# Issuing a state-space part's on-chip copies from ScalarE's queue instead of the sync engine's

## The chip, the cores and the metric

The kernel runs on one core of a Trainium2 chip. TensorE (PE) multiplies matrices into PSUM; VectorE (DVE), ScalarE (ACT) and GpSimd (POOL) do the elementwise work; SyncE (SP) computes nothing and here issues transfers. Every engine has an instruction queue of its own that it takes in order, and they meet only at semaphores. The metric is the time of one execution on the device in microseconds (us), the median of three runs.

## The reference, cut to what matters

The input is x of shape (8, 256, 128) after normalisation over the last axis. Two branches start from it and are multiplied at the end:

```python
xn = layernorm(x)
s = mamba_block(xn)                     # selective state space, D = 256 channels, N = 16 states
g = silu(local_transformer(xn))         # 6 layers, 16 heads, windows of 32 tokens, gelu feed-forward
x = x + s * g

# inside mamba_block, for each batch entry
delta = softplus(dbc[:DTR] @ dup_W + dup_b)
A_disc = exp(delta[..., None] * A)
B_x = delta[..., None] * Bm[:, :, None, :] * x1[..., None]
hc = A_disc[t] * hc + B_x[t]            # over 256 time steps
y = einsum('tbdn,btn->btd', hs, Cm)
```

## The kernel before, in words

There are 48 attention steps s: six layers over eight batch entries, each of 256 tokens. The loop `for i in STEADY` (i = 1 to 46) is written once for every engine, as a list of calls in a fixed order; a call such as `copy_p(i, 2)` works on step i and waits on semaphores for what it needs. A call whose step is not in range does nothing.

The state-space part is spread over the same loop. It works on one batch entry in every six steps (`is_batch`: s = 0, 6, ..., 42), eight in all. Its calls stand in the list at fixed lags, so that `z_bu(i - 3, 0)` acts only in steps i = 3, 9, 15, ..., 45. For one batch the sequence is:

- ACT copies the projections to `dbc` (`z_copy_dbc`), and POOL makes `du`, which holds delta and delta times x1 (`z_delta`).
- `replicate_bc(s, 0)` copies four groups of eight rows of `dbc` (the B and C rows) into partitions 0 to 7 of `BC`; `replicate_bc(s, 1)` to `(s, 4)` double them to 16, 32, 64 and 128 partitions. Each of these waits for the one before.
- `replicate(s, n)`, n = 0 to 7, copies sixteen rows of `du` into one of four buffers `rep`, each row into eight partitions. It waits for `delta_done` and, where the buffer was used before, until the decays and products that read it are done.
- Sixteen chunks j follow, two from each replication: ACT makes the decay `exp(delta A)` (`z_decay`), POOL the product with B (`z_bu`, line 1862), DVE the scan (`z_scan`), POOL the product with C (`z_hc`), PE the sum (`z_sum`). Chunk 0 of POOL also waits for all of `BC`.

In the kernel before, all transfers are on SP's queue. `spread` (line 539) copies pieces of V and `arrange_x` (line 553) rearranges x for the values; both wait for ACT or PE. The `replicate` and `replicate_bc` calls stand among them.

Of the attention part these calls bear on what follows, all in the order of the engine's list. On PE: `turn` and `turn_p` transpose q, k and the probabilities (`turn_p`, line 775, waits for POOL's `normalise_p`), `scores` and `values_out` use them, `w_gelu` and `w_gate` are the feed-forward products. On ACT: `copy_qk`, `copy_p`, `copy_o` and `copy_v` empty PSUM, `square` and `expo` feed the norms and the softmax, `gelu` feeds the feed-forward part. On POOL: `rotate_sum`, `normalise` and `normalise_p`. POOL's list for a step in which a batch starts has, near its end,

```python
z_bu(i - 3, 0)
z_bu(i - 3, 1)
rotate_sum(i + 1, 5)
normalise_p(i, 2)
z_bu(i - 3, 2)
rotate_sum(i + 1, 6)
z_bu(i - 3, 3)
normalise_p(i, 3)
```

with calls between them that do nothing in that step.

Of the kernel before, what the change touches and what calls it, by code (L numbers as in the profile page):

```python
# [21 lines left out]
NB, SEQ, DM = 8, 256, 128  # L22
# [354 lines left out]
def main_phase(nc, t, k, R2, T, C0, X, M, Y):  # L377

    with ExitStack() as ctx:
# [145 lines left out]
        def _(sp):  # L525
# [72 lines left out]
            def replicate_bc(s, n):  # L598

                if not is_batch(s):  # L600
                    return
                b = s // BSTEP
                if n == 0:
                    sp.wait_ge(dbc_copied, b + 1)
                    if b > 0:
                        sp.wait_ge(hc_done, 16 * b)
                    for z in range(2):
                        for h in range(2):
                            r = DTR + z * NST + 8 * h
                            sp.dma_start(BC[0:8, z, h, :], dbc[r:r + 8, :]).then_inc(bc_in, 16)  # L610
                else:
                    sp.wait_ge(bc_in, BC_IN * b + 64 + 16 * (n - 1))
                    r = 8 << (n - 1)
                    sp.dma_start(BC[r:2 * r], BC[0:r]).then_inc(bc_in, 16)

            def replicate(s, n):

                if not is_batch(s):
                    return
                b = s // BSTEP  # L620
                sp.wait_ge(delta_done, b + 1)
                k = 8 * b + n - NREP
                if k >= 0:
                    chunks = 16 * (k // 8) + 8 * (k % 8 // 4) + 5 + k % 4
                    sp.wait_ge(dA_done, chunks)
                    sp.wait_ge(bu_done, chunks)
                r = ROWS16[n]
                sp.dma_start(rep[:, (8 * b + n) % NREP].rearrange("p z c t -> p (z c t)"),
                             du[r::8].rearrange("d (o z) c t -> d o (z c t)", o=1).broadcast_to([16, 8, 2 * DBLK * SEQ]))\
                  .then_inc(rep_in[(8 * b + n) % NREP], 16)  # L630

# [12 lines left out]
            for i in STEADY:  # L644
                replicate(i - 6, 6)
# [3 lines left out]
                replicate(i - 3, 1)  # L649
# [3 lines left out]
                replicate_bc(i - 3, 0)  # L653
                replicate_bc(i - 3, 1)
                next_qk(i + 1, 0)
                replicate(i - 3, 2)
                replicate_bc(i - 3, 2)
                replicate_bc(i - 3, 3)
                replicate(i - 2, 0)
# [1441 lines left out]
```

## Time and profile before

| what | value |
|---|---|
| median of three runs | 1753.79 us (1752.3 to 1754.01) |
| the profiled execution's own time | 1751.25 us |
| span of the profile | 1749.2 us |
| PE busy | 1683.9 us, 96% |
| DVE busy | 1525.0 us, 87% |
| POOL busy | 1406.8 us, 80% |
| ACT busy | 1251.7 us, 72% |
| mean share of TensorE's clock granted | 0.994 |

The span runs from the first instruction to the last of the profiled execution; its own time includes what lies around it. Busy time of an engine counts its arithmetic; semaphores and the issuing of transfers are not in it. PE's busy time is a modelled one, since its matmuls are pipelined.

### The profile page before, as it was taken

The page shows a single profiled execution, that of the slowest core. Times are in us where ns is not written, and L with a number is a line of the kernel's source. Part 1 is how long each engine was busy: PE and PEld are TensorE (multiplying, and loading weights), DVE is VectorE, ACT ScalarE, POOL GpSimd, SP SyncE. Part 2 cuts the span into 40 slices and gives each one's busy share as a digit, 9 for nine tenths or more (in the row PEclk, how much of TensorE's full clock was granted, in tenths as well). Part 3 has the DMA queues.
Part 4 walks back from the last instruction along what each step waited for, and adds up shares of the span by engine and source line. Part 5 has one row for each costly group of instructions (what it writes and reads, how often), then busy time and mean ns, then how long its engine had stood idle before and what let it go on. Part 6 is the DMA issues. An engine that isn't in the chain of part 4 may idle for free.

```text
span 1749.2 us, 73908 instructions
## 1 busy us (share of the span) xinstructions
PE 1683.9 (96%) x30944; PEld 980.9 (56%) x30944; DVE 1525.0 (87%) x2751; ACT 1251.7 (72%) x2328; POOL 1406.8 (80%) x1265
## 2 busy tenths in 40 slices
PE   5899999999999999999999999999999999999987
PEld 2555555555556555555555555555555565556552
DVE  7878898989988999889889898898898989988976
ACT  4657677677786777866877668767677677786764
POOL 3777888878888887988889778897888888888872
PEclk9999999999999999999999999999999999999998
DMA  5213232232213322132421323214231242212340
GB/s 141 49 36 85 61 79 54 63 84 53 62 36 84 80 66 54 34 90 54 102 65 35 83 52 75 75 37 94 48 83 30 64 107 66 48 36 54 75 96 24
DMA packets 96694, 114.18 MB, mean 65 GB/s; under 512 B 42398, under 2 KB 62636, under 8 KB 96364
## 3 DMA queue, kind: packets, MB, share of 16 engines
q1 hardware_dynamic: 96364, 109.46, 26.3%
q8 instruction: 246, 4.03, 1.0%
q14 instruction: 84, 0.69, 0.1%
HBM read 19.22 MB, written 1.05 MB: 12 GB/s over the span
## 4 chain that ended last, share of the span: by engine, by line
PE 72%; DVE 14%; issue 4%; POOL 3%; SPq 2%; ACT 2%; DMA 2%; POOLq 0%; DVEq 0%; ACTq 0%
PE bank L713 14%; PE bank L797 9%; PE bank L738 9%; PE bank L729 8%; PE bank L814 7%; PE bank L758 6%; PE bank L775 5%; PE bank L842 3%; PE bank L857 3%; DVE qn L1490 3%; DVE qc L1490 3%; PE bank L866 2%; DVE ssq L1497 2%; PE bank L750 2%; PE bank L921 2%
## 5 line engine op out<-in xcount | busy, mean ns | idle before, releaser
L1817 POOL TENSOR_TENSOR AB<-qc,qn 128x512 f32<-128x512 f32 x384 | 487.9, 1276 | 116.7 <-DVE qn L1490 115.4
L1828 POOL TENSOR_TENSOR AB<-AB,rinv 128x512 f32<-128x512 f32 x384 | 392.0, 1045 | 31.8 <-DVE rinv L1515 31.8
L713 PE MATMUL bank<-wqkv,XT 128*128 128x512 f32 x768 | 380.2, 596 | 7.1 <-DVE qn L1490 4.9
L1835 POOL TENSOR_TENSOR Pb<-Pb,p_rden 128x512 f32<-128x512 f32 x192 | 200.8, 1046 | 144.0 <-DVE p_rden L1536 141.6
L1127 ACT ACTIVATE qkT<-bank 128x512 f32<-128x512 f32 x384 | 228.8, 596 | 107.3 <-PE bank L738 105.6
L1118 ACT ACTIVATE sq<-bank 128x512 f32<-128x512 f32 x384 | 228.5, 595 | 95.7 <-PE bank L713 95.5
L1490 DVE TENSOR_TENSOR qc<-bank,rt 128x512 f32<-128x512 f32 x384 | 258.6, 673 | 9.2 <-ACT sq L1118 7.3
L1497 DVE TENSOR_REDUCE ssq<-sq 128x8 f32<-128x512 f32 x384 | 258.1, 673 | 6.0 <-ACT sq L1118 5.2
L1490 DVE TENSOR_TENSOR qn<-bank,rt 128x512 f32<-128x512 f32 x384 | 261.5, 681 | 0.0
L797 PEld LDWEIGHTS bank<-PT,V 64*64 64x64 f32 x12288 | 196.9, 134 | 94.4 <-issue 89.8
L738 PE MATMUL bank<-ident,AB 128*128 128x128 f32 x1536 | 242.7, 280 | 3.7 <-ACT qkT L1127 3.3
L738 PEld LDWEIGHTS bank<-ident,AB 128*128 128x128 f32 x1536 | 173.7, 140 | 123.0 <-issue 85.1
L797 PE MATMUL bank<-PT,V 64*64 64x32 f32 x12288 | 217.9, 220 | 4.3 <-ACT PT L1142 2.4
L1142 ACT ACTIVATE PT<-bank 128x512 f32<-128x512 f32 x192 | 114.1, 594 | 147.1 <-PE bank L775 144.8
L1522 DVE TENSOR_REDUCE mx<-bank 128x8 f32<-128x512 f32 x192 | 131.2, 684 | 93.2 <-PE bank L758 92.5
L729 PE MATMUL bank<-wqkv,XV 128*128 128x512 f32 x384 | 191.2, 599 | 2.4 <-DVE qn L1490 2.4
L1605 DVE TENSOR_TENSOR_SCAN hb<-bank,hb 128x256 f32<-128x256 f32 x256 | 161.4, 672 | 33.3 <-ACT bank L1302 33.3
L814 PE MATMUL bank<-OT,wo 128*128 128x512 f32 x384 | 180.6, 593 | 0.0
L1862 POOL TENSOR_TENSOR hb<-rep,BC 128x512 f32<-128x512 f32 x128 | 163.3, 1282 | 12.2 <-DMA rep<-du 4.3
L713 PEld LDWEIGHTS bank<-wqkv,XT 128*128 128x128 f32 x768 | 127.1, 191 | 79.2 <-issue 68.3
L758 PE MATMUL bank<-qkT 64*32 64x64 f32 x12288 | 164.0, 222 | 3.9 <-issue 3.9
L1134 ACT ACTIVATE Pb<-Pb 128x512 f32<-128x512 f32 x192 | 120.8, 629 | 59.2 <-DVE Pb L1525 58.9
(145 smaller groups left out, 2492.5 us busy)
## 6 DMA issues: line engine op xcount, KB each, us to landing
V<-V SPq DMA_DIRECT2D x672, 64.0 KB
rep<-du SPq DMA_DIRECT2D x64, 512.0 KB, 4.7
wqkv<-in_Wqkv SPq DMA_DIRECT2D x36, 256.0 KB, 3.2
XV<-XT SPq DMA_DIRECT2D x96, 64.0 KB, 2.1
wo<-in_Wo SPq DMA_DIRECT2D x6, 512.0 KB, 5.3
BC<-BC SPq DMA_DIRECT2D x8, 256.0 KB
w<-in_W SPq DMA_DIRECT2D x6, 341.0 KB, 4.5
xin<-in_x SPq DMA_DIRECT2D x4, 256.0 KB, 4.1
```

The source lines that it names most:

```text
L713: pe.matmul(R[u % 2][:], XT[:, s % NB, (u % 2) * P:(u % 2 + 1) * P], wqkv[:, (u // 2) * 512:(u // 2 + 1) * 512], start=True, stop=True).th ...
L729: pe.matmul(R[n % 2][:], XV[:, q % 2, s % 2, tl, :], wqkv[:, c:c + 512], start=True, stop=True)\
L738: mm = pe.transpose(T[:, c * P:(c + 1) * P], AB[:, (8 * s + u) % NAB, c * P:(c + 1) * P], ident[:])
L758: mm = pe.matmul(SB[w * WIN:(w + 1) * WIN, odd, col:col + 2 * WIN], qkT[p0:p0 + DH, g % 2, c, WIN + tok:2 * WIN + tok], qkT[p0:p0 + DH, g ...
L797: mm = pe.matmul(o_bank(s)[DH * odd:DH * (odd + 1), tl, c * P + w * WIN:c * P + (w + 1) * WIN], V[r, w, h0:h0 + DH], PT[r, g % 2, 2 * odd ...
L814: mm = pe.matmul(c_bank("w_out", s), wo[:, k, :], flat(OT[:, k]), start=k == 0, stop=k == 7)
L1118: act.activation(sq[:, u % 2, :], R[u % 2][:], ACT.Square).then_inc(sq_done, 1)
L1127: act.activation(qkT[:, g % 2, :, WIN + tl * P:WIN + (tl + 1) * P], T.rearrange("p (c t) -> p c t", c=4), ACT.Copy).then_inc(qkT_done, 1)
L1490: ins = dve.tensor_tensor(out if z == 0 else out[:, :, :, ::-1, :], src, tab, ALU.mult)
L1497: dve.reduce_sum(ssq[:, 8 * u:8 * u + 8, 0], sq[:, u % 2, :].rearrange("p (h d) -> p h d", d=DH), AX_X)\
L1817: pool.tensor_tensor(AB[:, n % NAB, :], qc[:, u % 2, :], qn[:, u % 2, :], ALU.add).then_inc(rs_done, 1)
L1828: pool.tensor_tensor(o, o, r, ALU.mult).then_inc(nm_done, 1)
```

## The change

The functions `replicate_bc` and `replicate` move from SP's block to ACT's, with `sp` replaced by `act` and nothing else altered. Their calls leave SP's list and are placed in ACT's list, at the positions shown; the waits that they begin with are now in ACT's queue. The lists of PE, DVE and POOL are unchanged.

```diff
 SP's loop
             for i in STEADY:
-                replicate(i - 6, 6)
                 next_qk(i, 1)
                 next_qk(i, 2)
                 spread(i, 0)
-                replicate(i - 3, 1)
                 next_v(i, 0)
                 next_qk(i, 3)
                 spread(i, 1)
-                replicate_bc(i - 3, 0)
-                replicate_bc(i - 3, 1)
                 next_qk(i + 1, 0)
-                replicate(i - 3, 2)
-                replicate_bc(i - 3, 2)
-                replicate_bc(i - 3, 3)
-                replicate(i - 2, 0)
-                replicate(i - 6, 7)
                 spread(i, 2)
-                replicate_bc(i - 3, 4)
                 spread(i, 3)
                 arrange_x(i + 1)
-                replicate(i - 5, 5)
-                replicate(i - 4, 4)
-                replicate(i - 3, 3)
                 next_v(i, 1)
                 other_weights(i)
 ACT's block
+            def replicate_bc(s, n):
+
+                if not is_batch(s):
+                    return
+                b = s // BSTEP
+                if n == 0:
+                    act.wait_ge(dbc_copied, b + 1)
+                    if b > 0:
+                        act.wait_ge(hc_done, 16 * b)
+                    for z in range(2):
+                        for h in range(2):
+                            r = DTR + z * NST + 8 * h
+                            act.dma_start(BC[0:8, z, h, :], dbc[r:r + 8, :]).then_inc(bc_in, 16)
+                else:
+                    act.wait_ge(bc_in, BC_IN * b + 64 + 16 * (n - 1))
+                    r = 8 << (n - 1)
+                    act.dma_start(BC[r:2 * r], BC[0:r]).then_inc(bc_in, 16)
...
 ACT's loop
                 copy_v(i, 2)
+                replicate(i - 6, 6)
                 z_decay(i - 8, 14)
                 copy_v(i, 3)
                 z_decay(i - 5, 5)
                 copy_qk(i, 2)
                 expo(i, 0)
+                replicate(i - 3, 1)
                 square(i + 1, 0)
                 copy_qk(i, 3)
                 z_tap(i + 2)
                 z_decay(i - 6, 9)
                 scale_x(i - 3)
                 square(i + 1, 1)
+                replicate_bc(i - 3, 0)
                 z_copy_dbc(i - 1)
                 z_decay(i - 8, 15)
                 copy_p(i, 0)
                 square(i + 1, 2)
+                replicate_bc(i - 3, 1)
                 expo(i, 1)
                 gelu(i - 3, 0)
                 copy_qk(i, 4)
                 square(i + 1, 3)
+                replicate(i - 3, 2)
                 gelu(i - 3, 1)
                 copy_qk(i, 5)
+                replicate_bc(i - 3, 2)
                 copy_o(i, 0)
                 square(i + 1, 4)
                 gelu(i - 3, 2)
                 z_copy_g(i - 4)
+                replicate_bc(i - 3, 3)
                 z_decay(i - 4, 3)
                 copy_p(i, 1)
                 square(i + 1, 5)
+                replicate(i - 6, 7)
                 expo(i, 2)
                 copy_qk(i, 6)
+                replicate_bc(i - 3, 4)
                 square(i + 1, 6)
                 z_copy_dx(i - 1)
                 copy_o(i, 1)
+                replicate(i - 2, 0)
                 copy_qk(i, 7)
...
                 z_decay(i - 4, 4)
+                replicate(i - 5, 5)
                 z_softplus(i - 1)
                 copy_p(i, 2)
+                replicate(i - 4, 4)
                 expo(i, 3)
                 z_decay(i - 3, 0)
+                replicate(i - 3, 3)
```

After the loop the last batch's `replicate` calls 5, 6 and 7 move likewise, behind `copy_qk(LAST, 5)`, `copy_qk(LAST, 7)` and `expo(LAST, 3)`.

## Rows read from the trace of the kernel before

**Rows 1.** The profile page: busy time by engine, and the chain's shares.

```profile
PE 1683.9 (96%) x30944; PEld 980.9 (56%) x30944; DVE 1525.0 (87%) x2751; ACT 1251.7 (72%) x2328; POOL 1406.8 (80%) x1265
...
PE 72%; DVE 14%; issue 4%; POOL 3%; SPq 2%; ACT 2%; DMA 2%; POOLq 0%; DVEq 0%; ACTq 0%
```

**Rows 2.** POOL's waits: engine, line, waited for: us in total, times, longest.

```profile
POOL hb L1862 <- DMA rep<-du: 4.3, 5, 1.3
...
POOL hb L1862 <- DMA BC<-BC: 2.0, 1, 2.0
```

**Rows 3.** Instructions of tiles rep and BC: ns min/median/max, first and last start.

```profile
L628 SPq DMA_DIRECT2D rep<-du x64: 529/572/1876, 117.5 to 1696.1; - x64
...
DMA to landing us min/median/max: 4.3/4.7/5.9
...
L610 SPq DMA_DIRECT2D BC<-dbc x32: 624/649/1146, 142.2 to 1614.2; - x32
```

**Rows 4.** Busy time by engine in step 21: stretch, its length, us busy, clock.

```profile
769.20:803.20 34.00, 33.74 (x645) 19.98 (x646) 29.15 (x53) 26.05 (x47) 26.75 (x25) 1.00 0.45 99
```

**Rows 5.** SP's timeline, end of step 21: start us, us, instruction.

```profile
785.00 0.59 SPq L614 DMA_DIRECT2D BC<-BC  x1
...
792.79 0.56 SPq L628 DMA_DIRECT2D rep<-du  x1
```

**Rows 6.** Instructions of tile BC in step 21: first and last start.

```profile
L610 SPq DMA_DIRECT2D BC<-dbc x4: 624/644/682, 772.3 to 774.4; - x4
L614 SPq DMA_DIRECT2D BC<-BC x4: 507/608/1551, 776.2 to 785.0; - x4
```

**Rows 7.** POOL's timeline, end of step 21, with idle time before and releaser.

```profile
788.67 2.53 POOL L1862 TENSOR_TENSOR hb<-rep,BC 128x512 f32<-128x512 f32 x2 [0.73 <-issue]
...
792.36 1.06 POOL L1835 TENSOR_TENSOR Pb<-Pb,p_rden 128x512 f32<-128x512 f32 x1
...
797.18 1.27 POOL L1862 TENSOR_TENSOR hb<-rep,BC 128x512 f32<-128x512 f32 x1 [1.29 <-DMA rep<-du]
798.46 1.04 POOL L1835 TENSOR_TENSOR Pb<-Pb,p_rden 128x512 f32<-128x512 f32 x1
```

**Rows 8.** Line 1141's semaphore (the first wait of copy_p) on ACT's queue, 774 to 780.

```profile
L1141 ACTq EVENT_SEMAPHORE  x1: 17/17/17, 775.4 to 775.4; - x1
```

**Rows 9.** ACT's timeline in step 21.

```profile
776.53 0.59 ACT L1118 ACTIVATE sq<-bank 128x512 f32<-128x512 f32 x1
777.68 0.60 ACT L1142 ACTIVATE PT<-bank 128x512 f32<-128x512 f32 x1 [0.56 <-PE bank L775]
...
779.03 0.62 ACT L1134 ACTIVATE Pb<-Pb 128x512 f32<-128x512 f32 x1
...
780.97 0.69 ACT L1200 ACTIVATE ge<-bank,vecs 128x512 f32<-128x512 f32 x1
...
789.52 0.60 ACT L1127 ACTIVATE qkT<-bank 128x512 f32<-128x512 f32 x1 [0.38 <-PE bank L738]
...
795.45 0.60 ACT L1142 ACTIVATE PT<-bank 128x512 f32<-128x512 f32 x1 [1.96 <-PE bank L775]
796.66 0.63 ACT L1134 ACTIVATE Pb<-Pb 128x512 f32<-128x512 f32 x1 [0.62 <-DVE Pb L1525]
797.20 0.86 ACT L1302 ACTIVATE bank<-rep,Aneg 128x256 f32<-128x256 f32 x2
```

**Rows 10.** PE's timeline in step 21.

```profile
781.71 1.12 PE L842 MATMUL bank<-xc,w 128*128 128x512 f32 x2
...
794.75 0.66 PE L775 MATMUL bank<-ident,Pb 128*128 128x128 f32 x4
...
799.84 0.66 PE L775 MATMUL bank<-ident,Pb 128*128 128x128 f32 x4
```

**Rows 11.** Two stretches early in the span: length, us busy, clock as in rows 4.

```profile
97.30:100.70 3.40, 1.30 (x66) 1.22 (x67) 2.79 (x8) 2.25 (x7) 1.04 (x1) 1.00 0.10 23
100.70:104.10 3.40, 3.40 (x8) 1.80 (x8) 0.12 (x1) 1.68 (x3) 3.20 (x4) 0.50 0.25 59
```

More of the change, by code:

```diff
@@ L596, in store @@
                              written(p).rearrange("p (i n) -> p i n", n=DM)).then_inc(stored, 16)
[L598 to L630, printed above, removed]
             def take_state():
@@ L674, in _ @@
             spread(LAST, 3)
-            replicate(LAST_B, 5)
-            replicate(LAST_B, 6)
-            replicate(LAST_B, 7)
             reload_x()
@@ L1161, in copy_v, with replicate @@
                    .then_inc(v_copied, 1)
+            def replicate_bc(s, n):
[14 more added lines that the diff above has]
+                    act.dma_start(BC[r:2 * r], BC[0:r]).then_inc(bc_in, 16)
+            def replicate(s, n):
+                if not is_batch(s):
+                    return
+                b = s // BSTEP
+                act.wait_ge(delta_done, b + 1)
+                k = 8 * b + n - NREP
+                if k >= 0:
+                    chunks = 16 * (k // 8) + 8 * (k % 8 // 4) + 5 + k % 4
+                    act.wait_ge(dA_done, chunks)
+                    act.wait_ge(bu_done, chunks)
+                r = ROWS16[n]
+                act.dma_start(rep[:, (8 * b + n) % NREP].rearrange("p z c t -> p (z c t)"),
+                             du[r::8].rearrange("d (o z) c t -> d o (z c t)", o=1).broadcast_to([16, 8, 2 * DBLK * SEQ]))\
+                  .then_inc(rep_in[(8 * b + n) % NREP], 16)
             def guess_q(s, h=0):
@@ L1429, in _ @@
             copy_qk(LAST, 5)
+            replicate(LAST_B, 5)
             z_decay(LAST_B, 6)
@@ L1435, in _ @@
             copy_qk(LAST, 7)
+            replicate(LAST_B, 6)
             z_decay(LAST_B, 7)
@@ L1439, in _ @@
             expo(LAST, 3)
+            replicate(LAST_B, 7)
             z_decay(LAST_B, 8)
```

## The prediction

> **What bounds the kernel now.** I read the profile page first. PE is busy 96% of the span, and the chain that ended last runs over PE for 72% of its length, over DVE for 14%, over DMA and over SP's queue for 2% each [rows 1]. So a microsecond counts when it stops PE, and ACT, busy 72%, matters only through what it hands on. The list of waits came second: POOL's first product of the state-space part (line 1862) waits five times, 4.3 us in all, on the replicated copies, and 2.0 us once on the BC rows [rows 2]. Third, the rows of the moved transfers [rows 3]: an issue occupies SP's queue for about 0.6 us, and a replication lands 4.7 us after its issue begins.
>
> Then I took one batch apart, the fourth (s = 18). What matters happens in step i = 21, from 769.2 to 803.2 us. Within these 34.00 us PE is busy 33.74 [rows 4], so there is almost nothing in which a delay could disappear. In this step the BC rows reach POOL only just in time: its first product z_bu(18, 0) starts at 788.67 after 0.73 us of idling, and the last BC stage was issued at 785.00. The fourth product waits too: POOL idles 1.29 us and starts it at 797.18, when the replication issued at 792.79 has landed [rows 5, 7]. POOL takes its queue in order: behind the first product stands normalise_p(21, 2), behind the fourth normalise_p(21, 3). PE turns their results at 794.75 and 799.84, which is 1.3 and 0.3 us after POOL finishes them (792.36 + 1.06 and 798.46 + 1.04) [rows 7, 10].
>
> **What the change does, part by part.** Each batch has 16 issues: four BC rows out of dbc, four doublings of BC, eight replications. With eight batches that is 128 issues, and at 0.57 to 0.65 us each [rows 3] some 78 us of queue time go from SP to ACT.
>
> *Taken from SP.* SP loses 78 us of issuing and its waits on the decays. What remains there is V, XV and the weights, and the chain gives SP's queue 2%; I count the gain as nothing. Its bound is what POOL waits on the moved transfers now: 0.73 + 1.29 = 2.0 us in a batch like the fourth [rows 7].
>
> *Added to ACT, the plain issue.* An issue stands between two activations of about 0.6 us each. If ACT's queue starts it only when the activation before it ends, it costs 0.6 us; if the queue runs ahead of the arithmetic, it disappears under the activation that is running. The trace speaks for the second: the semaphore that copy_p(21, 0) waits for was passed at 775.4, while the copy itself ran at 777.68, and square(22, 1), which stands before it in the queue, started only at 776.53 [rows 8, 9]. The Trainium skill ("TensorE: Matmul & The Clock Gate", Engine queue depths) gives ScalarE a strict first-in first-out queue of eight; the rows agree that it is deeper than one. A lone replication costs ACT between 0 and 0.6 us, and I take 0. Of the replications only number 3 is short of time; the others come later than now too, but POOL asks for them later still. I take 0 for them and leave their issues to a rival.
>
> *Term A: the four issues in a row, and the first doubling behind them.* replicate_bc(18, 0) stands behind square(22, 1). Its four issues take 4 x 0.65 + 3 x 0.04 = 2.7 us. From 775.4, where the queue already is, they end at 778.1, and copy_p(21, 0), now at 777.68, moves by 0.4. The first doubling then waits on ACT until the fourth row has landed. On SP that took from 774.4 to 776.2, 1.8 us [rows 6]. The fourth issue begins at 775.4 + 3 x 0.69 = 777.5, so it lands at 779.3; the doubling's issue ends at 779.9, and expo(21, 1), now at 779.03, moves by 0.9. A table load and gelu(18, 0) follow without a gap, and PE's next product for the feed-forward part, at 781.71, starts 0.05 us after that gelu ends (780.97 + 0.69) [rows 9, 10]. PE is late by 0.9. Without running ahead the issues start at 776.5, and the term is 2.0; if issuing from ACT were nearly free it would be near 0.
>
> *Term B: BC is complete later.* The last doubling is issued behind copy_qk(21, 6): 789.52 + 0.9 = 790.4, where SP did it at 785.00. Landing then takes 788.67 - 785.00 = 3.7 us, so BC is complete at 794.1 and z_bu(18, 0) moves by 5.4. normalise_p(21, 2) ends at 798.8 instead of 793.4. PE wants its result at 794.75 + 0.9 = 795.65, so it stops for 3.15 us and is now 4.05 us late. Bounds: 1.3, if the piece lands in the 1.8 us of the small rows; 4.2, if the doublings before it are late by a further microsecond. I take the value from the stage itself.
>
> *Term C: replication 3 is issued later.* It stands behind expo(21, 3) and z_decay(18, 0), and these behind copy_p(21, 2), which needs the transposition that PE just did 4.05 us late. copy_p moves from 795.45 to 799.5; the queue passes the next three instructions at once, so the issue is at 799.6 (now 792.79) and lands 4.7 us later, at 804.3. z_bu(18, 3) takes 1.27 us and normalise_p(21, 3) 1.04, to 806.6. PE now starts there at 799.84: it is 6.8 us late, of which 2.7 are new. Bounds: 2.3 to 3.9, with the shortest and the longest landing of [rows 3], 4.3 and 5.9.
>
> The sum is 0.9 + 3.15 + 2.7 = 6.75 us a batch. The order is the same in all eight, and the times at which PE asks and ACT issues hang on their own order, so I take 8 x 6.75 = 54 us. In batches where POOL does not wait now it has something to spare, but the spare time is POOL's, not PE's. The last batch's final three replications also move a few microseconds, in the tail; I count nothing.
>
> *The clock.* PE will stand still for about 3 us twice a batch. In the trace a stretch of 3.40 us with PE busy 1.30 ran at the full clock (2.4 GHz) and the following 3.40 us at half of it (1.2 GHz) [rows 11]. One such stretch costs at most 1.7 us, so one a batch up to 14 us. After the stop of term B PE waits again anyway, so only the second could be felt. I leave it out of the likeliest sum and keep it in the range.
>
> The profiled execution took 1751.25 us (span 1749.2 and 2.05 around it), 2.5 below the median of 1753.79. 1751.25 + 54 = 1805; on the scale of the median 1808.
>
> **The rivals.**
>
> *Slower, but more cheaply: BC is not late.* If transfers on ACT's queue land sooner because no V piece stands ahead of them, or ACT gets to the doublings earlier than I think, A and B vanish and C alone remains: replication 3 issued at 796.7, right behind the start of expo(21, 3) [rows 9], landed at 801.4, normalise_p done at 803.7, PE 3.9 late, 31 us in all, 1785. For it: the longest issue on SP took 1.9 us [rows 3], so its queue did stop at times. Against: five stages each wait on the one before, and the last stands behind copy_qk(21, 6) whatever they do.
>
> *Much slower: ACT pays every issue.* If ACT's queue does not pass an issue while an activation runs, A is 2.0, C 0.9 more (the issue waits for the decay), and seven more replications cost 0.57 each: 6 us a batch more, 48 in all, of which I let half fall into ACT's waits for PE: 1832. With the clock's 14 us on the forecast instead: 1822. Against: the early semaphore [rows 8].
>
> *No change: the transfers are hidden anyway.* As a mechanism of this kernel it needs POOL to have more than 5 us to spare before its two normalise_p; the rows show 1.3 and 0.3. It would give 1754. The Trainium skill ("DMA: Bandwidth & Descriptors", Issuing engines are not separate DMA queues) says that all issuers share the same 16 DMA engines and that a second issuer saves only sequencer time; by that rule alone SP saves time that nobody waits for, and nothing moves.
>
> *Faster: SP was what made BC and replication 3 late.* Today V pieces stand on SP between the moved ones. If ACT issued them before 785.0 and 792.8, POOL's waits would go: 6.3 us by the list [rows 2], 16 if all batches were like the fourth, 1738 to 1747. It decides where ACT reaches copy_qk(21, 6) and z_decay(18, 0): 789.5 and 797.2 [rows 9], both later than SP's issues. That speaks plainly against it.
>
> **How the numbers follow.** A change of 0.2% is about what a measurement of this kernel can tell from none. Chances: the forecast (1790 to 1826) 0.55, the cheaper one 0.2, the much slower one 0.15, no change 0.06, faster 0.04. So slower 0.90, same 0.06, faster 0.04. The range goes from a little under the cheaper case, 1772, to a little over the much slower one, 1838.
>
> **What would show it.** Right: eight waits of POOL's line 1862 on replications, of about 3 us, and eight on BC; new waits of PE at its transposition of Pb (line 775) on POOL; steps i = 3, 9, 15 and so on longer by about 7 us and the others unchanged; issues on ACT's queue that start while an activation still runs. Wrong: no such waits of POOL (then BC and replication 3 came early), all steps of a batch longer by a little (then ACT pays each issue), or a half-clock stretch in each of these steps (then the clock is a term). The prediction falls if the time from issue to landing on ACT's queue is far from 4.7 us, or if the doublings are not what POOL waits for.

## The result, and the profile after

The changed kernel takes 1816.7 us (median of four runs, 1815.69 to 1822.19), the kernel before 1753.05 in the same series: a ratio of 1.0367, interval 1.0352 to 1.0383. It is slower by 64 us, where 54 were forecast. The profiled execution of the changed kernel took 1817.19 us, with a span of 1815.1. One of the four executions of the kernel with replication 3 alone (below) took 2144.58 us at a mean granted clock of 0.749 and is left out of its time.

The page first, busy time by engine (PEld are TensorE's weight loads) and the chain's shares, answering to [rows 1]:

```profile
PE 1702.8 (94%) x30944; PEld 989.8 (55%) x30944; DVE 1527.3 (84%) x2751; ACT 1252.1 (69%) x2328; POOL 1406.1 (77%) x1265
...
PE 70%; DVE 11%; issue 8%; POOL 4%; ACT 2%; ACTq 1%; DMA 1%; POOLq 0%; DVEq 0%
```

The span grew by 65.9 us. PE's busy time grew by 18.9 with the same 30944 matmuls, so 47.0 us are new idle time and 18.9 are matmuls that ran slower. ACT's and POOL's busy times did not change: nobody got more work. The queue that carried it shows in the chain only as ACTq 1%; what it did shows as "issue" (4% before, 8% now) and POOL (3%, now 4%).

The waits of the changed kernel, answering to [rows 2] (engine, line, waited for: us in total, times, longest):

```profile
PE bank L725 <- POOL Pb L1835: 36.6, 17, 3.9
POOL hb L1862 <- issue: 36.1, 7, 6.2
...
POOL hb L1862 <- DMA rep<-du: 27.9, 8, 5.0
...
PE bank L792 <- ACT ge L1184: 12.5, 8, 2.5
...
POOL hb L1862 <- DMA BC<-BC: 4.8, 1, 4.8
...
PE bank L747 <- ACT PT L1092: 4.5, 10, 0.9
```

PE's lines have moved up by 50: L725 is the transposition of the probabilities (775 before), L747 `values_out` (797), L792 the feed-forward product (842). POOL's product with B (line 1862) waits eight times, 27.9 us, on a replication, and eight times, 36.1 + 4.8 us, on BC; the view names seven of these "issue", because it shows nothing that they waited for, and the experiment that moves BC alone shows whose they are. PE's wait for POOL's probabilities went from 3.0 us in three waits to 36.6 in 17. PE's waits for gelu, 12.5 us in eight, are new; those for copy_p grew from 2.4 to 4.5 us.

The transfers themselves, tiles rep and BC, answering to [rows 3]:

```profile
L1143 ACTq DMA_DIRECT2D rep<-du x64: 536/541/615, 125.0 to 1762.6; - x64
...
DMA to landing us min/median/max: 4.2/4.4/6.1
...
L1125 ACTq DMA_DIRECT2D BC<-dbc x32: 631/711/1564, 143.6 to 1665.1; - x32
```

A replication lands after 4.4 us from ACT's queue, 4.7 from SP's. The transfers did not get slower; they are issued later.

Now the step that the prediction took apart, i = 21, from 790.54 to 831.82 us, and the last batch's and the tail (stretch, its length, us busy of PE, PEld, DVE, ACT and POOL, clock, DMA share, GB/s), answering to [rows 4]:

```profile
790.54:831.82 41.28, 35.61 (x650) 20.75 (x654) 29.44 (x53) 25.90 (x47) 27.75 (x26) 0.96 0.37 82
1656.04:1703.03 46.99, 37.11 (x646) 21.84 (x646) 29.89 (x54) 26.09 (x48) 29.33 (x27) 0.93 0.32 72
1737.80:1815.10 77.30, 56.91 (x764) 29.13 (x762) 44.13 (x72) 37.32 (x69) 33.73 (x30) 0.86 0.24 57
```

Step 21 took 34.00 us before and takes 41.28 now. From the starts of copy_qk(i, 0) the eight steps i = 3, 9, ..., 45 together are 62.3 us longer (277.25 before, 339.59 now); the other 38 steps changed by 1.6 us in all; the tail from copy_qk(47, 0) to the end went from 71.5 to 77.3.

PE's timeline in step 21, answering to [rows 10], shows where its 5.67 us of idle time lie (in brackets, with the releaser):

```profile
801.12 1.14 PE L747 MATMUL bank<-PT,V 64*64 64x32 f32 x64 [0.40 <-ACT PT L1092]
...
805.23 1.13 PE L792 MATMUL bank<-xc,w 128*128 128x512 f32 x2 [1.53 <-ACT ge L1184]
...
821.03 0.76 PE L725 MATMUL bank<-ident,Pb 128*128 128x128 f32 x4 [2.68 <-POOL Pb L1835]
821.58 1.92 PE L679 MATMUL bank<-wqkv,XV 128*128 128x512 f32 x2
823.29 3.50 PE L816 MATMUL bank<-ge,w 128*128 128x512 f32 x6
...
828.91 0.63 PE L725 MATMUL bank<-ident,Pb 128*128 128x128 f32 x4 [1.06 <-POOL Pb L1835]
```

The first two stops are term A (1.93 us; 0.9 forecast), the third term B (2.68; 3.15), the last term C (1.06; 2.7). Between B and C, PE works slowly: the pair at line 679 takes 1.92 us where it took 1.02, the six products at 816 take 3.50 where they took 2.74.

POOL in the same step, answering to [rows 7]:

```profile
816.16 2.50 POOL L1862 TENSOR_TENSOR hb<-rep,BC 128x512 f32<-128x512 f32 x2 [4.91 <-issue]
...
819.85 1.03 POOL L1835 TENSOR_TENSOR Pb<-Pb,p_rden 128x512 f32<-128x512 f32 x1
...
826.49 1.28 POOL L1862 TENSOR_TENSOR hb<-rep,BC 128x512 f32<-128x512 f32 x1 [3.15 <-DMA rep<-du]
827.72 1.05 POOL L1835 TENSOR_TENSOR Pb<-Pb,p_rden 128x512 f32<-128x512 f32 x1
```

PE starts at 821.03, 0.15 us after POOL's 819.85 + 1.03, and at 828.91, 0.14 after 827.72 + 1.05: the transposition now waits for POOL both times, and POOL for a transfer. ACT's timeline, answering to [rows 9], with the issues on its queue (ACTq) between the activations:

```profile
795.48 0.54 ACTq L1143 DMA_DIRECT2D rep<-du  x1
...
796.84 0.72 ACTq L1125 DMA_DIRECT2D BC<-dbc  x1
797.18 0.81 ACT L1177 ACTIVATE xc<-xc,vecs 128x512 f32<-128x512 f32 x1
797.59 1.46 ACTq L1125 DMA_DIRECT2D BC<-dbc  x1
797.89 0.58 ACT L1068 ACTIVATE sq<-bank 128x512 f32<-128x512 f32 x1
799.08 1.29 ACTq L1125 DMA_DIRECT2D BC<-dbc  x2
800.47 0.60 ACT L1092 ACTIVATE PT<-bank 128x512 f32<-128x512 f32 x1 [2.00 <-issue]
...
801.87 0.63 ACTq L1129 DMA_DIRECT2D BC<-BC  x1
802.55 0.63 ACT L1084 ACTIVATE Pb<-Pb 128x512 f32<-128x512 f32 x1 [0.99 <-DMA BC<-dbc]
...
813.05 0.51 ACTq L1129 DMA_DIRECT2D BC<-BC  x1
...
822.03 0.58 ACTq L1143 DMA_DIRECT2D rep<-du  x1
```

The first row's issue begins at 796.84, 1.05 us before square(22, 1) (797.89) that stands ahead of it in the list: the queue does run ahead of the arithmetic. But four issues in a row use that up, and copy_p(21, 0) stands 2.00 us idle behind them. The first doubling then waits until 801.87 for the rows, and expo(21, 1) another 0.99 behind it.

### The profile page after: what moved, and what is told of

The parts are those of the page before. It is cut to its first block, busy times and chain, and to the rows that moved or that the text cites. A ratio compares the mean times of both kernels' runs of the same rounds, so it can differ in the third digit from the quotient of the medians.

```text
span 1815.1 us, 73908 instructions
## 1 busy us (share of the span) xinstructions
PE 1702.8 (94%) x30944; PEld 989.8 (55%) x30944; DVE 1527.3 (84%) x2751; ACT 1252.1 (69%) x2328; POOL 1406.1 (77%) x1265
## 3 DMA queue, kind: packets, MB, share of 16 engines
HBM read 19.22 MB, written 1.05 MB: 11 GB/s over the span
## 4 chain that ended last, share of the span: by engine, by line
PE 70%; DVE 11%; issue 8%; POOL 4%; ACT 2%; ACTq 1%; DMA 1%; POOLq 0%; DVEq 0%
PE bank L663 13%; PE bank L747 9%; PE bank L688 9%; PE bank L679 8%; PE bank L764 6%; PE bank L708 5%; PE bank L725 5%; PE bank L792 3%; PE bank L807 3%; PE bank L816 3%; DVE qn L1490 2%; DVE qc L1490 2%; PE bank L700 2%; DVE ssq L1497 2%; PE bank L871 2%
## 5 line engine op out<-in xcount | busy, mean ns | idle before, releaser
L1497 DVE TENSOR_REDUCE ssq<-sq 128x8 f32<-128x512 f32 x384 | 258.2, 673 | 17.7 <-ACT sq L1068 16.9
L747 PEld LDWEIGHTS bank<-PT,V 64*64 64x64 f32 x12288 | 198.7, 135 | 100.2 <-issue 86.6
L747 PE MATMUL bank<-PT,V 64*64 64x32 f32 x12288 | 220.0, 221 | 9.0 <-ACT PT L1092 4.5
L1862 POOL TENSOR_TENSOR hb<-rep,BC 128x512 f32<-128x512 f32 x128 | 163.0, 1279 | 73.7 <-issue 36.1
L679 PE MATMUL bank<-wqkv,XV 128*128 128x512 f32 x384 | 196.6, 614 | 0.6 <-DVE qn L1490 0.6
L725 PE MATMUL bank<-ident,Pb 128*128 128x128 f32 x768 | 126.9, 289 | 38.9 <-POOL Pb L1835 36.6
```

What stands on the lines that cost most here:

```text
L679: pe.matmul(R[n % 2][:], XV[:, q % 2, s % 2, tl, :], wqkv[:, c:c + 512], start=True, stop=True)\
L747: mm = pe.matmul(o_bank(s)[DH * odd:DH * (odd + 1), tl, c * P + w * WIN:c * P + (w + 1) * WIN], V[r, w, h0:h0 + DH], PT[r, g % 2, 2 * odd ...
L1497: dve.reduce_sum(ssq[:, 8 * u:8 * u + 8, 0], sq[:, u % 2, :].rearrange("p (h d) -> p h d", d=DH), AX_X)\
```

## The experiments

Each ratio is set against the kernel before on the same chip and in the same series (1751.39 to 1753.05 us); times of different series differ by up to 1.7 us from that alone.

| kernel | us | ratio, with its interval |
|---|---|---|
| the change | 1816.7 | 1.0367 (1.0352 to 1.0383) |
| replications on ACT, BC on SP | 1794.53 | 1.0247 (1.0229 to 1.0265) |
| BC on ACT, replications on SP | 1799.37 | 1.0273 (1.0255 to 1.0292) |
| replication 3 alone on ACT | 1796.62 | 1.0248 (1.0219 to 1.0276) |
| before, with 128 small issues added on ACT | 1761.49 | 1.0060 (1.0039 to 1.0081) |
| the change, replication 1 back on SP | 1810.77 | 1.0336 (1.0315 to 1.0357) |
| the change, POOL's list reordered | 1781.74 | 1.0163 (1.0137 to 1.0189) |
| before, POOL's list reordered | 1763.78 | 1.0062 (1.0037 to 1.0086) |
| all on ACT, at earlier places | 1768.20 | 1.0099 (1.0079 to 1.0119) |
| all on ACT, rows a step earlier | 1758.51 | 1.0034 (1.0023 to 1.0046) |
| the same, last three replications on SP | 1753.31 | 1.0011 (0.9998 to 1.0024) |
| the change, last three replications on SP | 1810.88 | 1.0344 (1.0331 to 1.0358) |

### The two halves of the change

Replications alone (SP keeps `replicate_bc` where it was):

```diff
 SP's loop
-                replicate(i - 6, 6)
...
-                replicate(i - 3, 3)
 ACT's loop
+                replicate(i - 6, 6)
...
+                replicate(i - 3, 3)
```

> The replications are issued from ACT as after the change, the BC transfers from SP as before it. Theory (three stops of PE in a row in the step in which a batch starts): the first two stops (the four rows and the first doubling in ACT's queue, and BC complete too late) are gone, the third stays: replication 3 is issued behind expo(i, 3), some 4 us later than from SP, and PE stops 3.6 us at its transposition of the last probabilities. 8 x 3.6 = 29 us over the kernel before: about 1782. Rival (ACT pays for every issue): half of the issues, half of the loss, spread over the steps in which replications are issued: 1785, but with steps i = 2, 4, 5, 6 of a batch longer too. Rival (transfers on a second queue land late): replications land in clearly more than 4.4 us, POOL waits in other steps as well.

BC alone (SP keeps `replicate`):

```diff
 SP's loop
-                replicate_bc(i - 3, 0)
...
-                replicate_bc(i - 3, 4)
 ACT's loop
+                replicate_bc(i - 3, 0)
...
+                replicate_bc(i - 3, 4)
```

> The other half: the BC transfers are issued from ACT as after the change, the replications from SP as before it. Theory: the first two stops stay, 1.9 and 2.7 us by the profile after the change, the third is gone: 8 x 4.6 = 37 us over the kernel before, about 1790, and POOL's waits on replications are as before or gone. Together with the other half this should come to more than the whole change (29 + 37 = 66 against 64), or to about as much. Rival (ACT pays for every issue): 64 issues of the 128, 1785, spread.

Measured 1794.53 and 1799.37, that is 42 and 47 us above before. Each half costs more than expected, and together they would make 89, not 64. What the expectations lacked is the clock. In the eight steps i = 3, 9, ..., 45 PE's idle time grew by 27.3 us with the replications alone (29 expected) and by 31.4 with BC alone (37 expected), but its work took 10.6 and 14.4 us longer; and with the replications alone the tail took 74.0 us instead of 71.5. With BC alone, these waits remain in the view of waits:

```profile
POOL hb L1862 <- issue: 38.4, 7, 6.6
...
PE bank L752 <- POOL Pb L1835: 26.0, 10, 4.4
...
PE bank L819 <- ACT ge L1195: 8.1, 8, 1.5
```

So POOL's "issue" waits are those on BC. With the replications alone there are such waits too, though BC is still on SP:

```profile
POOL hb L1862 <- issue: 17.2, 7, 3.7
```

Before, they were 2.6 us in four. In step 21 the last doubling of BC is issued 16.9 us after the step's start (15.8 before) and POOL's z_bu(18, 0) starts at 20.86 (19.47 before); in steps 3, 9, 27 and 45 PE stops for this, by 0.37 to 1.68 us. So the second stop was not gone everywhere, as the expectation had it. Replication 1 is in flight now when the first doubling is issued (5.1 and 5.5 us into the step; before, replication 1 came before the step began). That this is what delays the doublings was not tried. In step 21 PE's timeline has one stop left, and what follows it runs at half speed (four products of line 702 took 3.00 us, 1.98 before):

```profile
817.43 1.08 PE L748 MATMUL bank<-ident,Pb 128*128 128x128 f32 x4 [4.55 <-POOL Pb L1835]
818.31 3.00 PE L702 MATMUL bank<-wqkv,XV 128*128 128x512 f32 x4
```

### One transfer of sixteen: replication 3

```diff
 SP's loop
-                replicate(i - 3, 3)
 ACT's loop
                 z_decay(i - 3, 0)
+                replicate(i - 3, 3)
```

> The kernel before with replication 3 alone, the call behind z_decay(i - 3, 0), moved to ScalarE's queue: term C by itself, 8 transfers instead of 128. With all eight replications of a batch on ScalarE's queue the steps i = 3, 9, ... were 4.7 us longer, and the time 42 us. If replication 3 is the only one of them that matters in the loop, as the prediction says, those steps are 4.7 us longer here too and the time is about 1752 + 38 = 1790. If the seven others carry a part of it, the steps are longer by the forecast 2.7 us of term C, and the time is about 1752 + 22 = 1774.

Measured 1796.62, some 7 above the first theory: eight transfers of the 128 cost 45 us, and the seven other replications of a batch, which the first experiment moved too, cost nothing on top (1794.53 with them). The second theory falls. The timelines of ACT, POOL and PE in step 21 of this kernel:

```profile
815.15 0.54 ACTq L1174 DMA_DIRECT2D rep<-du  x1
```

```profile
820.53 1.26 POOL L1878 TENSOR_TENSOR hb<-rep,BC 128x512 f32<-128x512 f32 x1 [6.30 <-DMA rep<-du]
821.75 1.04 POOL L1851 TENSOR_TENSOR Pb<-Pb,p_rden 128x512 f32<-128x512 f32 x1
```

```profile
822.94 1.08 PE L774 MATMUL bank<-ident,Pb 128*128 128x128 f32 x4 [4.74 <-POOL Pb L1851]
```

From issue to use it takes 5.4 us here, where it took 4.4 before (792.79 to 797.18) [rows 5, 7]. Step 21 takes 40.53 us, 6.5 more: 4.5 of new idle time (4.74 and nothing else, against 0.26) and 2.05 in which PE was slow (its busy time in the step went from 33.74 to 35.79). In all eight such steps together 31.2 us are new idle time and 14.7 slow work.

### The issues without their waits

The kernel before, with a transfer of 256 bytes into a tile that nobody reads added wherever the change puts an issue on ACT; the real transfers stay on SP.

```diff
+            def issue():
+
+                n = issued[0]
+                issued[0] += 1
+                act.dma_start(spare[16 * (n % 8):16 * (n % 8) + 16, n // 8, :], ident[0:16, 0:4]).then_inc(spare_in, 16)
...
                 expo(i, 0)
+                issue_rep(i - 3, 1)
...
                 square(i + 1, 1)
+                issue_bc(i - 3, 0)
...
```

> The kernel before, with all its transfers on SP, and 128 extra transfers of 256 bytes from a constant, issued from ACT at the 128 places where the changed kernel issues its own, without any wait; nobody uses their data. It prices the plain issue. Theory (the queue runs ahead and an issue disappears under the running activation, only the four in a row show): between 0 and 1.9 us in each of eight steps, 1753 to 1768. Rival (ACT pays every issue, 0.56 us each): 72 us less what falls into ACT's waits for PE, 1790 or more.

Measured 1761.49, 9.3 more. (The profiled execution was the longest of the four, 1766.89 us; 5.0 us of what it took more lie ahead of the loop and in the tail, where only three of the 128 issues stand.) The steps i = 3, 9, ... are 1.26 us longer on average; the stop is the one of term A, before the feed-forward product. In step 21, on PE's timeline:

```profile
790.58 1.12 PE L845 MATMUL bank<-xc,w 128*128 128x512 f32 x2 [1.05 <-ACT ge L1222]
```

ACT's timeline shows what made it:

```profile
786.21 1.64 ACTq L1172 DMA_DIRECT2D spare<-ident  x1
...
787.89 0.63 ACT L1137 ACTIVATE Pb<-Pb 128x512 f32<-128x512 f32 x1 [1.10 <-issue]
```

The four issues in the place of the rows moved copy_p(21, 0) by 0.46 us only (to 785.71, 8.94 us after the step's start; 8.48 before), as the forecast had it. The next issue, in the place of the first doubling, took 1.64 us, and expo(21, 1) stood behind it. SP issues a doubling at the same time (786.29); whether that makes it long was not tried. The steps that hold lone issues only (others than i = 3, 9, ...) are 0.8 us longer in all 38 together. So a lone issue is free there, and these five close together cost about a microsecond without any wait of their own.

### What stands ahead of the four rows

```diff
 SP's loop
                 spread(i, 0)
+                replicate(i - 3, 1)
 ACT's loop
                 expo(i, 0)
-                replicate(i - 3, 1)
                 square(i + 1, 0)
```

> The changed kernel with replication 1 alone, the call between expo(i, 0) and square(i + 1, 0), back on the sync engine's queue. In the changed kernel PE stopped 0.40 and 1.53 us in step 21 before its products behind copy_p(21, 0) and gelu(18, 0): term A, 1.9 us against the 0.9 forecast. If A is large because replication 1 stands ahead of the four rows in ACT's queue, those stops shrink to about 0.9 us, the BC stages that follow come earlier by the same, and the time falls by some 8 us to about 1809. If the four rows themselves are slow to issue from ACT, or the doubling behind them is late for its own sake, A stays at 1.9 us and the time at 1816.7.

Measured 1810.77, 6 us less than the whole change (4.4 less when each is set against the kernel before in its own series). The waits:

```profile
PE bank L742 <- POOL Pb L1851: 38.7, 18, 3.5
...
PE bank L809 <- ACT ge L1201: 8.0, 8, 1.4
```

PE's waits of term A fall from 12.5 to 8.0 us (and the grown part at `values_out` vanishes, 4.5 to 2.4), so A is 1.0 us a batch without replication 1 ahead of the rows, and 1.8 with it (12.5 + 2.1, by 8). The waits for POOL grew by 2.1 us at the same time: an earlier PE asks earlier, and then waits longer for a transfer. So the expected 1809 was nearly met, but not by the expected way. The first seven batch steps took 292.6 us in the profile of the change, 291.1 in this one and 289.7 in a kernel whose loop is that of the change (the last experiment): a shorter stop of term A did not show in their length. The 6 us came from the last batch's step, which took 46.99 us in the profile of the change, 41.85 in this one and 43.91 in that other kernel, and from the tail (77.3 and 74.5).

### Taking POOL's probabilities out from behind the products

```diff
 POOL's loop
+                z_bu(i - 4, 3)
                 z_bu(i - 4, 4)
...
-                z_bu(i - 3, 0)
...
-                z_bu(i - 3, 1)
...
                 rotate_sum(i + 1, 5)
...
                 normalise_p(i, 2)
-                z_bu(i - 3, 2)
...
                 rotate_sum(i + 1, 6)
+                z_bu(i - 3, 0)
+                z_bu(i - 3, 1)
+                z_bu(i - 3, 2)
...
-                z_bu(i - 3, 3)
...
                 normalise_p(i, 3)
```

In the changed kernel:

> The changed kernel, with nothing but POOL's order altered, and only in the steps around the start of a batch: products 0, 1 and 2 stand behind normalise_p(i, 2) and rotate_sum(i + 1, 6) instead of ahead of them, product 3 behind the first normalise calls of the next step. Transfers and ACT's order are those of the change. Theory (the late transfers cost because normalise_p stands behind the products that wait for them): the second and third stops of PE go, the first (1.5 to 1.9 us, ACT's own queue) stays: 8 x 1.5 to 1.9 = 12 to 15 us, 1765 to 1768. Rival (the loss is in ACT's queue or in the transfers as such): 1800 or more.

In the kernel before:

> The kernel before, all transfers on SP, with POOL's altered order. It asks whether the waits of POOL in the kernel before (0.7 and 1.3 us in a batch like the fourth) cost anything. Theory (PE asks for normalise_p 1.3 and 0.3 us after POOL has it, so POOL's waits are inside that slack): no change, 1749 to 1755. Rival (they are on the path, as the chain through SP's queue in the first and last batch says): up to 2 us a batch, 1738 to 1747.

Measured 1781.74 and 1763.78. Both are later than expected, by the same mistake: the reorder has a price of its own, 12 us on the kernel before, since the next step's first `normalise_p` comes later (7.67 us into step 22 for 6.52; PE waits 1.87 us at `values_out` in that step, which took 38.6 us for 36.5). Within the step that the reorder cures, the theory holds. Steps 21 and 22 of the reordered changed kernel, in the view of stretches:

```profile
779.86:815.85 35.99, 34.00 (x646) 20.01 (x646) 29.34 (x53) 26.14 (x47) 25.57 (x24) 1.00 0.42 94
815.85:853.50 37.65, 35.54 (x652) 21.38 (x653) 34.97 (x62) 24.29 (x49) 31.96 (x31) 1.00 0.25 63
```

Step 21 falls from 41.28 to 35.99 us, its clock is full again, and PE waits 4.4 us in the whole run for POOL's probabilities, as in the reordered kernel before (4.4). The last doubling of BC is issued as late as in the change (22.3 us into step 21, 22.5 there); PE no longer stands behind it. The two reordered kernels differ by 18 us. PE's waits for gelu, term A, are 11.8 of it; in the profiles the eight batch steps differ by 14.6 us and the tail by 2.4.

### Placing the same issues where they are early

All sixteen on ACT. First the rows one at a time at the step's start, the doublings 4 to 8 us and replication 3 11 us earlier in step 21 than in the change (the other doublings, and the places that the calls left, are cut here):

```diff
+                row_bc(i - 3, 0)
                 copy_qk(i, 1)
+                row_bc(i - 3, 1)
...
                 copy_v(i, 2)
+                row_bc(i - 3, 2)
...
                 copy_v(i, 3)
+                row_bc(i - 3, 3)
...
                 expo(i, 0)
+                replicate_bc(i - 3, 1)
...
                 square(i + 1, 5)
+                replicate(i - 3, 3)
...
```

> Everything is on ACT's queue as after the change, but at earlier places in the same step: the four rows one by one behind four activations at the start of the step, the doublings behind expo(i, 0), square(i + 1, 1), gelu(i - 3, 0) and copy_qk(i, 5), replication 3 behind square(i + 1, 5). Theory (it is the place in ACT's order, not ACT's queue, that costs): all three stops go, 1750 to 1760, like the kernel before. Rival (ACT's queue costs by itself, by its issues or by slower landings): most of the loss stays, 1790 or more.

Measured 1768.20, a miss of 8 us. Terms B and C are gone, but the first doubling now waits on ACT for its rows, ahead of copy_qk(i, 3), and PE waits for that. On PE's timeline in step 21:

```profile
784.27 0.30 PE L700 MATMUL bank<-maskb,identb 64*32 64x256 bf16 x8 [1.68 <-ACT qkT L1077]
```

Then the rows still earlier, in the step before, so that no doubling finds its input missing:

```diff
                 copy_qk(i, 1)
+                replicate_bc(i - 3, 1)
...
                 square(i + 1, 5)
+                replicate(i - 3, 3)
...
                 copy_v(i + 1, 0)
+                row_bc(i - 2, 0)
...
                 copy_p(i, 3)
+                row_bc(i - 2, 1)
                 copy_o(i, 2)
+                row_bc(i - 2, 2)
                 copy_v(i + 1, 1)
+                row_bc(i - 2, 3)
```

> All on ACT's queue as in the run with the earlier places, but the four rows stand in the last third of the step before, behind four separate activations, and every doubling stands where the one before has landed by the times of that run, so that nothing in ACT's queue waits for a transfer. That run lost 1.6 us a batch, with PE waiting for copy_qk behind the first doubling. Theory (an issue costs ACT only where it makes the queue wait, or where several stand together): the 1.6 us go too, 1749 to 1756. Rival (a lone issue costs ACT a few tenths of a microsecond): 16 to 20 us stay as in the earlier run, 1764 or more.

Measured 1758.51, 2 us above the expected range. The batch steps are back: 278.3 us for all eight, 277.25 before. What is left is in the tail, 77.41 us, with a stop of 1.79 at values_out(47, 1). So the last batch's three replications behind the loop went back to SP:

```diff
 SP, behind the loop
                 spread(LAST, 3)
+                replicate(LAST_B, 5)
+                replicate(LAST_B, 6)
+                replicate(LAST_B, 7)
 ACT, behind the loop
-                replicate(LAST_B, 5)
...
-                replicate(LAST_B, 6)
...
-                replicate(LAST_B, 7)
```

> The kernel with the BC rows a step earlier (1758.51 us) keeps the loop's steps at their old lengths, and what is left over before (about 6 us) lies behind the loop: from the start of copy_qk(47, 0) to the end it takes 77.4 us, 71.5 in the kernel before. Here the last batch's replications 5, 6 and 7, behind the loop, go back to the sync engine's queue; everything else stays on ScalarE's. If those three issues among copy_qk(47, 5) to expo(47, 3) make the tail late, it is 71.5 us again and the whole 1750 to 1753 us, a little less than before, since three of the eight batch steps are 1.6 us shorter. If the tail is long for another reason (the clock after the loop, or the transfers that the sync engine no longer has), it stays at 77 us and the time at 1758.

Measured 1753.31: 13 of a batch's 16 issues in the last batch, and all 16 in the others, come from ACT, and the time is that of the kernel before (ratio 1.0011, interval 0.9998 to 1.0024), 0.3 us above the expected range. A gain did not appear, although POOL's products with B wait for no transfer any more (4.3, 2.0 and 2.6 us in the kernel before): the eight batch steps took 276.2 us for 277.3, so those waits were worth next to nothing, and the rival "faster" of the prediction falls. The stop of 1.79 us is gone; the tail took 73.73 us in the profile, not 71.5, with PE's clock at 0.84 of full speed there.

The same edit on the changed kernel:

> The changed kernel with only the last batch's replications 5, 6 and 7, behind the loop, put back on the sync engine's queue. If the tail is a separate term that adds to the others, its 77.3 us become 71.5 and the time goes from 1816.7 to 1811. If it comes from the long step before it (the last batch's step takes 47.0 us there, with two half-clock stretches), the time stays within 1 us of 1816.7.

Measured 1810.88, as the first branch had it, and the tail is as before, in the view of stretches:

```profile
1734.26:1805.70 71.44, 53.07 (x764) 26.91 (x762) 44.26 (x72) 37.15 (x69) 33.74 (x30) 0.92 0.25 62
```

## Why the prediction was right, and where its sizes were off

**The mechanism** was right: a handful of issues became late because of what stands ahead of them on ACT, POOL waited, the probabilities behind POOL's products were late, and PE stopped. Reordering POOL removed those stops with BC as late as in the change; issuing the same transfers early from the same engine removed nearly the whole loss (1758.51 with all 128 on ACT). So neither ACT's share of the work nor the engine that issues is the cause, but the place in the order. The chance of 0.90 on slower was the right side, and the range held the time.

**The plain issue at 0** was right for a lone one (0.8 us in 38 steps with small transfers), and 0 was right for the seven replications other than number 3 when they moved without BC. The rival in which ACT pays every issue falls with the same runs.

**Term A** was mis-sized: 0.9 forecast, 1.93 in step 21 and 1.8 a batch. The four issues begin where the forecast had them, 6.3 us after the step's start (6.2 forecast). They were counted at 0.65 us each; the second one took 1.46 and the four together 3.5 instead of 2.7. With replication 1 back on SP they took 2.8 (0.72, 0.70 and 1.37 for two), and A was 1.0. The prediction moved replication 1 at no cost, since nobody waits for it, and did not ask who is queued behind it. Why a row issued behind it takes longer is open. Counted from the step's start, copy_p(21, 0) ran 1.45 us later than before (0.4 forecast) and expo(21, 1) 2.18 later (0.9 forecast): the wait of the first doubling for its rows was the smaller part.

**Term B** came out near (2.68 for 3.15) by errors that cancel. The issue was placed 0.9 us after copy_qk(21, 6) begins; it began with it, at 813.05. The landing was 3.1 us (813.05 to 816.16), not 3.7. That makes 1.5 less. But copy_qk(21, 6) itself came later by term A, 0.9 in the forecast, which had let PE move by it and ACT not. 3.15 - 1.5 + 0.9 = 2.55.

**Term C and the clock** belong together. From the transposition of step 21's third block to that of the fourth PE took 5.09 us before (794.75 to 799.84) and 7.88 now (821.03 to 828.91): 2.79 more, with 2.7 forecast. Only 1.06 of it is idle time. The rest is slow work: after the stop of term B the granted clock fell to half, 1.2 GHz of 2.4, over most of this stretch (length, us busy and clock as above), answering to [rows 11]:

```profile
820.50:824.50 4.00, 3.47 (x8) 1.93 (x9) 2.03 (x6) 2.64 (x7) 2.84 (x3) 0.61 0.33 74
```

The prediction said that such a piece after B would disappear in the next wait; it did, in step 21. Step 33 shows it without a sum. In the changed kernel PE stopped there for 2.75 us (B) and 0.97 (C), at a mean granted clock of 0.96, and the step took 41.18 us. In the kernel of the last experiment, whose loop is the same, the clock stayed full, the stops were 2.77 and 2.66, and the step took as long:

```profile
1222.08:1263.35 41.27, 33.92 (x650) 20.08 (x654) 29.44 (x53) 25.90 (x47) 27.74 (x26) 1.00 0.37 82
```

So 2.7 was the size of C at full clock. Step 21 closes: 5.67 idle - 0.26 idle before + 1.87 slow = 7.28 us, the whole growth from 34.00 to 41.28. But leaving the clock at 0 was not right for the whole run. A half-clock stretch in each of these steps was one of the prediction's signs that the clock is a term, and it came: the mean granted clock is 0.92 to 0.96 in each of the eight, 1.00 in each before. PE's work in them took 18.9 us longer (2.9 more in the tail are made up for in the other steps), while the stops of C were only 1.5 us a batch: together 3.9 a batch where 2.7 were forecast. In the last batch's step slow work (37.11 busy, 33.93 before) came on top of stops of 2.86 (A), 3.92 (B) and 3.10 (C), so that this step alone lost 12.8. That step took 43.91 us in the profile of the last experiment's kernel, so some 3 us of it vary between executions.

**The tail** was counted at nothing and is a term: 77.3 us for 71.5, and 4 to 6 us of the time when its three replications went back to SP (twice; the lower figure with each kernel set against the kernel before in its own series). Its size varies between the profiles: 73.3 to 77.5 us in the six kernels that issue these three from ACT, 71.5 or 71.6 in five that leave them on SP and put nothing else there, but 73.7 in the one with the early issues. How much is the stop of 1.8 us and how much the clock that fell behind it was not settled.

**The sum.** The batch steps grew by 62.3 us, 7.8 each, against 54 and 6.75; the tail by 5.8; the start and the other steps shrank by 2.2. That is the span's 65.9. By terms, the stops a batch were 1.8 (A), 2.8 (B) and 1.5 (C), the slow work 2.4, and 0.7 of idle time that these steps had before is gone: 7.8. So A and the clock were too small in the forecast and B and C too large, and 54 came as near as it did partly because these errors cancel. By steps, the first seven batches cost 7.1 each, close to the 6.75, and what was missing lies in the last batch's step (6 more than forecast) and in the tail (6).

**The rival "BC is not late"** had the right mechanism and a wrong price: term C alone was to cost 3.9 us a batch and give 1785. Replication 3 alone cost 45 us. The new idle time was what the rival said, 31.2 us or 3.9 a batch; what it lacked is the slow work behind the stop, 14.7 us or 1.8 a batch, which no second stop hides. (Its transfer landed after 4.6 to 5.3 us, median 4.7; step 21 has the longest.) In the whole change C is cheaper because the stop of B holds PE back while DVE and ACT prepare the next block. In the lone case replication 3 is issued 2.1 us after the transposition of the third block (815.15 and 813.04), since expo(21, 3), ahead of it, still waits for DVE; in the whole change DVE is done by then, and it is issued 1.0 us after it (822.03 and 821.03). With the slow work, which each half pays for itself (1.3 and 1.8 us a batch, 2.4 in the whole), this goes a good way to say why the halves, 42 and 47 us, do not add up to 64; that it is all of it was not shown.

**The rule on issuing engines** (the Trainium skill, "DMA: Bandwidth & Descriptors", Issuing engines are not separate DMA queues) has all issuers share the DMA engines. The runs agree as far as the time to landing goes: 4.4 us from ACT and 4.7 from SP. By itself the rule left "no change", 1754, and the version with early issues does end there. The 64 us lie in when each queue reaches its issue.

## What to carry to other kernels

Before a transfer's issue moves to another engine, find for each one the row that releases its user and how long that user can wait; here one transfer in sixteen, issued 4.1 us later in its step (27.68 us after the step's start for 23.59), cost 45 us when it was moved alone, and seven others like it cost nothing. Issue it behind work that does not depend on its users, one at a time, early enough that no issue in the queue has to wait for the landing of another. And look at what the late consumer has queued behind it: moving that out of the way removed the stops as well, but had a price of its own that only a run of the reordered kernel before could show. And count the slow work behind a stop as a term: it was 18.9 of the 62 us that the batch steps grew by.

## What the runs showed of the hardware

In each of the eight batch steps of the changed kernel a part of PE's work ran at half the granted clock, 1.2 GHz of 2.4, most often from about the end of the stop of some 2.7 us on (820.50 to 824.50 in step 21: 0.61 on the mean). Not every such stop was followed by one: in step 33 of the last experiment's kernel, with stops of 2.77 and 2.66 us, the clock stayed at 1.00. With replication 3 alone all eight stops (4.1 to 4.7 us) went with slow work, 1.8 us a batch on the mean (2.05 in step 21); where a second stop followed, the slow work took the place of a part of it (step 33 above).

An issue on ACT's queue can start before the activation ahead of it does (796.84 against 797.89 us), and a lone one cost nothing that the time shows. Several close together did cost: the four rows of the changed kernel moved the activation behind them by 1.45 us in step 21, and single issues took up to 1.56 us there and 1.64 with small transfers, instead of 0.65.
